# ScalarE norms the fifth tile's x one round sooner, and VectorE takes the sixth tile's statistics behind the shared expert's first activation

## The chip, the cores and the metric

The kernel runs on one core of a Trainium2 chip, in one launch. The metric is the time of an execution in microseconds of the device, the median of several runs. The engines are TensorE (PE, with its weight loads PEld), VectorE (DVE), ScalarE (ACT), GpSimd (POOL) and SyncE (SP), which issues DMAs. They run side by side and wait for each other by semaphores only.

## The reference

The input is x, 16 sequences of 512 tokens, 128 wide, in float32. Cut to what is computed:

```python
y  = layernorm(x)                                  # no gain
n1 = layernorm(y) * ln1_g + ln1_b
r, k, v = sigmoid(n1 @ Wr.T), n1 @ Wk.T, n1 @ Wv.T
e   = exp(k - exp(n1 @ Ww.T))
num = scan(decay * num + e * v);  den = scan(decay * den + e)   # along the sequence
a   = y + (r * num / (den + eps)) @ Wo.T
n2  = layernorm(a) * ln2_g + ln2_b
x1  = x + a + sigmoid(n2 @ Wrec.T) * (relu(n2 @ Wkey.T) ** 2 @ Wval.T)
h   = layernorm(x1)
out = x1 + shared_expert(h) + routed_expert(h)     # 1 of 16 experts for each token
```

## The kernel before

A tile is one sequence of 512 tokens, so there are 16 tiles, in four groups of 128 tokens. The first part of the kernel, some 330 us, takes all tiles through the time mix, the channel mix, the router and the shared expert, and scatters the rows by expert into HBM. The second part runs the routed experts on the sorted rows and isn't touched.

In the first part each engine has one program of rounds, `one_round(n)`. In round n the line `for t in at(k)` runs its step for tile t = n - k, so one round holds steps of several tiles, each at its own stage, in an order that is written out by hand. Rounds of different engines are not aligned by anything but the semaphores: `wait(engine, name, t)` waits until the step called `name` is done for tile t. An engine that waits holds back all that is written behind it.

The steps in question, with the lines of the profile, are these.

- VectorE, `stats_of_x(t)`: the mean and variance of x by four BATCH_NORM_STATS2 (L1180, into `stA`) and four BATCH_NORM_AGGREGATE (L1185, into `mvA`). It waits for the load of x. Tiles 0 to 3 are done ahead of the rounds, tile 4 (`EARLY_STATS`) early in round 4, the later ones at `at(0)`, between `so_far` and `ev`.
- GpSimd, the terms of the norm (`pA`, L1650 to L1656), one group of small instructions, first in its round at `at(2)`. Behind them in the same round come `row_ids`, `h_terms` (L1603, L1590, L1592, L1606: the terms of the norm of h, for an older tile), `scaled` (L1616, h times the router's score), the four products `p1`, `p3`, `p0`, `p2` (L1672 to L1678), `xn0`, `sum_a`, `pC` and the scatters (L1630). In the round with `pA(5)`, `h_terms` is of tile 1, `scaled` of tile 0 and the products of tile 3.
- ScalarE, `norm_x(t)`: four activations (L935), one for each group, which write `xn1tok`. It stands second in its round, behind `tanh_of_max`. Later in the round come `copy_a`, `silu1`, `copy_x`, the four `relu`, `gate_tanh`, `norm_h` (L1010), `exp_w` (L1004, behind a load of the table), `copy_h` (L1016) and more. `norm_x(2)` is moved already: it stands behind `exp_w(1)`.
- TensorE, `turn_x(t)`: the transposes of `xn1tok` (L429), which wait for `norm_x(t)`. In the same round follow `gate1`, `up1` (which waits for `ev`), `keys`, `down_first`, `last_key` (L560, which waits for `act1` of the tile two back), the projections of x, `turn_h` (L429 too), the products with Wo (L734 to L745, each of which waits for one of `p1`, `p3`, `p0`, `p2`), `gate0`, `logits`, `up0`, the products with Wval (L435) and at the end the transposes of `an` (L781).
- VectorE in round 5, in order: `norm_a(2)`, the scan of `den(3)` (L1421), `so_far(0)`, `stats_of_x(5)`, `ev(3)` (L1431), `q(3)` (L1436), `act0(0)` (L1333), `mixed(1)` (L1339 to L1343, with the statistics of h), a reciprocal, `act1(0)` (L1354), a reciprocal, the scan of `num(3)` (L1455) and two reciprocals. Round 6 begins with `places(0)` and `k_less_w(4)` (L1274), which waits for `exp_w(4)`.

Of the kernel before, what the change touches and what calls it, by code (L numbers as in the profile page):

```python
# [93 lines left out]
def program(nc, x, w_main, w_exp, vecs, out):  # L94
# [4 lines left out]
    with ExitStack() as ctx:  # L99
# [12 lines left out]
        def wait(eng, name, t, k=None):  # L112

            of = WHO.get(name, range(NT))
            count = sum(1 for u in of if u <= t)
            if count:
                eng.wait_ge(s[name], (count - 1) * PER[name] + (PER[name] if k is None or t not in of else k))
# [88 lines left out]
        def grp(tile, g):  # L206
            return tile[:, g * P:(g + 1) * P]
# [20 lines left out]
        def at_round(n):  # L228


            return lambda behind, of=range(NT): [n - behind] if n - behind in of else []
# [6 lines left out]
        EARLY_STATS, IN_HALVES = 4, 2  # L238
# [630 lines left out]
        def _(act_e):  # L869
# [23 lines left out]
            def tanh_of_max(t):  # L893
                wait(act_e, "mx", t)
                wait(act_e, "sc", t - 2)
                af(ths[t % 2][:, :], mx[t % 2][:, :], ACT.Tanh, scale=0.5).then_inc(s["ths"], 1)
# [19 lines left out]
            def silu1(t):  # L916
                wait(act_e, "G1", t)
                wait(act_e, "ac1", t - 1)
                af(sgA[1][:, :], bank[4][:, :], ACT.Silu).then_inc(s["sg1"], 1)

            def copy_a(t):
                if t < IN_HALVES:
                    for half in range(2):
                        wait(act_e, "T2", t, half + 1)
                        af(xn2T[t % 2][:, half * HALF:(half + 1) * HALF], T2_of(t, half)[:, half * HALF:(half + 1) * HALF], ACT.Identity,
                           bias=V("b2"), scale=V("g2")).then_inc(s["xn2T"], 1)
                else:
                    wait(act_e, "T2", t)
                    af(xn2T[t % 2][:, :], T2_B[:, :], ACT.Identity, bias=V("b2"), scale=V("g2")).then_inc(s["xn2T"], 2)  # L929

            def norm_x(t):
                wait(act_e, "pA", t)
                wait(act_e, "T1", t - 2)
                for g in range(G if t else 1):
                    ins = af(grp(xn1tok[t % 2], g), grp(xin[t % XR], g), ACT.Identity, bias=smA[t % 3][:, 5, g:g + 1],  # L935
                             scale=smA[t % 3][:, 4, g:g + 1])
                ins.then_inc(s["xn1tok"], 1)

            def copy_x(t):
                act_e.wait_ge(s["T1"], t + 1)  # L940
                af(xn1T[t % 2][:, :], T1_B[:, :], ACT.Identity, bias=V("b1"), scale=V("g1")).then_inc(s["xn1T"], 1)

            def exp_r(t):
                act_e.wait_ge(s["Rp"], t + 1)
                wait(act_e, "q", t - 2)
                af(er[t % 2][:, :], R_B[:, :], ACT.Exp, scale=-1.0).then_inc(s["er1"], 1)
# [9 lines left out]
            def relu0(t):  # L956
                act_e.wait_ge(s["K0"], t + 1)
                wait(act_e, "k20", t - 1)
                af(kr[0][:, :], KE_BANK[0][:, :], ACT.Relu).then_inc(s["kr0"], 1)

            def relu2(t):
                wait(act_e, "K2", t)
                wait(act_e, "k22", t - 1)
                af(kr[2][:, :], KE_BANK[2][:, :], ACT.Relu).then_inc(s["kr2"], 1)

            def relu1(t):
                wait(act_e, "K1", t)
                wait(act_e, "k21", t - 1)
                af(kr[1][:, :], KE_BANK[1][:, :], ACT.Relu).then_inc(s["kr1"], 1)

            def relu3(t):
                wait(act_e, "K3", t)
                wait(act_e, "k23", t - 1)
                af(kr[3][:, :], KE_BANK[3][:, :], ACT.Relu).then_inc(s["kr3"], 1)  # L974

            def square0(t):
                wait(act_e, "kr0", t)
                wait(act_e, "VAL0", t - 1)
                af(k2[0][:, :], kr[0][:, :], ACT.Square).then_inc(s["k20"], 1)
# [16 lines left out]
            def gate_tanh(t):  # L996
                wait(act_e, "REC", t)
                wait(act_e, "rv", t - 2)
                af(th[t % 2][:, :], REC_B[:, :], ACT.Tanh, scale=0.5).then_inc(s["th"], 1)

            def exp_w(t):
                wait(act_e, "Wp", t)
                wait(act_e, "e", t - 2)
                af(ew[t % 2][:, :], W_B[:, :], ACT.Exp).then_inc(s["ew"], 1)  # L1004
# [18 lines left out]
            def one_round(n):  # L1023
                at = at_round(n)
                for t in at(6):
                    tanh_of_max(t)
                for t in at(2):
                    if t != 2:
                        norm_x(t)
                for t in at(4):  # L1030
                    copy_a(t)
                    if t == 0:
                        exp_r(t + 2)
                for t in at(6, A_TILES):
                    silu1(t)
                for t in at(6, B_TILES):
                    wait(act_e, "hG0", t)
                    wait(act_e, "hac0", t - 1)
                    af(sgB[0][:, :], bank[2][:, :], ACT.Silu).then_inc(s["hsg0"], 1)
                for t in at(2):  # L1040
                    if t != 2:
                        copy_x(t)
                for t in at(6, B_TILES):
                    wait(act_e, "hG1", t)
                    wait(act_e, "hac1", t - 1)
                    af(sgB[1][:, :], bank[4][:, :], ACT.Silu).then_inc(s["hsg1"], 1)
                for t in at(4):
                    relu0(t)
                    relu2(t)
                    relu1(t)  # L1050
                    gate_tanh(t)
                for t in at(4):
                    if t == 1:
                        relu3(t)
                        square0(t)
                for t in at(2):
                    if t == 3:
                        exp_w(t)
                for t in at(5):
                    norm_h(t)  # L1060
                for t in at(2):
                    if t - 4 in A_TILES:
                        nc.scalar.preload_act_table(ACT.Exp)
                    if t not in (2, 3):
                        exp_w(t)
                    if t == 1:
                        norm_x(t + 1)
                for t in at(5):
                    copy_h(t)
                for t in at(4):  # L1070
                    if t != 1:
                        relu3(t)
                        square0(t)
                for t in at(2):
                    if t != 1:
                        exp_z(t)
                for t in at(4):
                    square2(t)
                for t in at(2):
                    if t == 1:  # L1080
                        copy_x(t + 1)
                    if t != 2:
                        exp_r(t)
                for t in at(4):
                    square1(t)
                for t in at(2):
                    one_more(t)
                    if t == 1:
                        exp_w(t + 1)
                        exp_z(t)  # L1090
                for t in at(4):
                    square3(t)
                for t in at(5, A_TILES):
                    silu0(t)
# [69 lines left out]
        def _(dve):  # L1164
# [97 lines left out]
            def stats_of_x(t):  # L1262
                dve.wait_ge(s[f"x_in{t % XR}"], 16 * (t // XR + 1))
                wait(dve, "agA", t - 2)
                bn_stats_of(stA[t % 2], lambda g: grp(xin[t % XR], g), "agA")
                wait(dve, "agA", t, 1)
                wait(dve, "pA", t - 3)
                wait(dve, "xn1tok", t - 3)
                bn_aggr_of(mvA[t % 3], stA[t % 2], "agA")
# [60 lines left out]
            def act0(t):  # L1330
                wait(dve, "sg0", t)
                wait(dve, "U0", t)
                v.tensor_tensor(actA[0][:, :], sgA[0][:, :], bank[3][:, :], ALU.mult).then_inc(s["ac0"], 1)  # L1333
# [36 lines left out]
            def one_round(n):  # L1370
                at = at_round(n)
# [50 lines left out]
                for t in at(5):  # L1422
                    so_far(t)
                for t in at(0):
                    if t > EARLY_STATS:
                        stats_of_x(t)
                for t in at(2):
                    wait(dve, "e", t)
# [7 lines left out]
                    v.scalar_tensor_tensor(q[t % 2][:, :], den[t % 2][:, :], WKV_EPS, er[t % 2][:, :], ALU.add, ALU.mult).then_inc(s["q"], 1)  # L1436
                for t in at(5, A_TILES):
                    act0(t)
                for t in at(4):
                    mixed(t)  # L1440
                for t in at(2):
# [328 lines left out]
```

## Time and profile before

| | |
|---|---|
| median of 3 runs | 484.36 us (484.09 to 484.52) |
| the profiled execution, its time | 484.58 us |
| the profiled execution, its span | 482.9 us |
| PE busy | 472.7 us, 98% |
| DVE, ACT, POOL busy | 371.4, 324.2 and 352.6 us |

The span is that of the instructions; the execution's own time holds 1.68 us more around it. A busy PE is not PE at its peak, since matmuls are pipelined. The chain of work that ended last lies on PE for 84% of the span. Times in rows are counted from the start of the span. A releaser in brackets is the instruction whose end let the waiting one start.

### The profile page before, as it was taken

The numbers are of one execution on the slowest core, as the hardware profiler recorded it, in microseconds if no ns is written. First come the engines' busy times: TensorE is split into PE (matmuls) and PEld (weight loads), VectorE is DVE, ScalarE is ACT, GpSimd is POOL, SyncE is SP. The second block draws the span as 40 slices with busy tenths as digits, with TensorE's granted clock in tenths as the row PEclk, the third lists the DMA queues.
The fourth block names the chain that finished last, engine by engine and source line by source line (L and its number), as shares of the span: only waits on it lengthen the run. The fifth ranks groups of instructions, "written<-read, shape, count | busy, mean of one in ns | idle before, by whom it ended". The sixth has DMA issues, their size and how long they took to land.

```text
span 482.9 us, 10368 instructions
## 1 busy us (share of the span) xinstructions
PE 472.7 (98%) x3025; PEld 383.6 (79%) x3025; DVE 371.4 (77%) x1076; ACT 324.2 (67%) x625; POOL 352.6 (73%) x571
## 2 busy tenths in 40 slices
PE   8999999999999999999999999999999999999997
PEld 7556677868777778686777868877889999999996
DVE  7899899999999999996899989847545455555426
ACT  2777887987978879777687986563265555565421
POOL 6667498898898988986798877767326777767750
PEclk9999999999999999999999999999999999999999
DMA  7052001102102011010101001011489855542028
GB/s 240 2 191 115 1 23 44 56 12 67 34 33 68 23 45 56 12 66 24 44 24 46 33 12 46 33 42 39 121 187 246 229 167 150 150 130 72 23 68 282
DMA packets 33031, 39.32 MB, mean 81 GB/s; under 512 B 4913, under 2 KB 29113, under 8 KB 32720
## 3 DMA queue, kind: packets, MB, share of 16 engines
q1 hardware_dynamic: 26640, 24.98, 18.1%
q0 software_dynamic: 5760, 13.16, 7.8%
q8 instruction: 25, 0.41, 0.4%
q10 hardware_dynamic: 576, 0.52, 0.3%
q14 instruction: 30, 0.25, 0.2%
HBM read 21.69 MB, written 17.93 MB: 82 GB/s over the span
## 4 chain that ended last, share of the span: by engine, by line
PE 84%; DVE 6%; issue 3%; DMA 2%; ACT 2%; POOL 2%; SPq 1%; DVEq 0%; POOLq 0%; ACTq 0%
PE bank L442 20%; PE bank L435 11%; PE bank L459 6%; PE bank L450 4%; PE bank L850 4%; PE bank L858 3%; PE bank L857 3%; PE bank L548 3%; PE bank L560 3%; PE bank L544 3%; PE bank L539 3%; PE bank L429 3%; PE bank L534 2%; PE bank L605 2%; PE bank L619 2%
## 5 line engine op out<-in xcount | busy, mean ns | idle before, releaser
L442 PE MATMUL bank<-hT,wm 128*128 128x256 f32 x512 | 124.7, 383 | 0.6 <-ACT kr L974 0.6
L442 PEld LDWEIGHTS bank<-hT,wm 128*128 128x128 f32 x512 | 92.0, 190 | 18.7 <-issue 8.5
L1630 POOL DMA_INDIRECT sorted_rows<-rows,posi x64 | 72.8, 1138 | 20.1 <-issue 16.9
L1725 POOL DMA_INDIRECT out<-shared x55 | 53.2, 967 | 36.2 <-DVE shared L1542 22.7
L435 PEld LDWEIGHTS bank<-wm,k 128*128 128x128 f32 x512 | 61.7, 192 | 8.0 <-issue 6.4
L435 PE MATMUL bank<-wm,k 128*128 128x128 f32 x512 | 62.4, 275 | 0.1
L1153 ACT ACTIVATE er<-bank 128x256 f32<-128x256 f32 x40 | 15.3, 383 | 41.6 <-PE bank L858 40.9
L1550 DVE TENSOR_TENSOR e<-er,bank 128x256 f32<-128x256 f32 x40 | 16.8, 421 | 22.5 <-ACT er L1153 18.9
L459 PE MATMUL bank<-wm,actA 128*128 128x128 f32 x240 | 32.9, 280 | 0.0
L1010 ACT ACTIVATE h<-rows,smE 128x128 f32<-128x128 f32 x64 | 26.3, 482 | 8.1 <-POOL smE L1606 8.0
L459 PEld LDWEIGHTS bank<-wm,actA 128*128 128x128 f32 x240 | 29.3, 192 | 0.2 <-issue 0.2
L1725 POOL DMA_INDIRECT out<-rows x24 | 23.2, 965 | 7.8 <-issue 5.2
L1683 POOL TENSOR_SCALAR shared<-shared,smA 128x128 f32<-128x128 f32 x64 | 27.9, 448 | 0.0
L935 ACT ACTIVATE xn1tok<-shared,smA 128x128 f32<-128x128 f32 x61 | 25.0, 481 | 2.8 <-POOL smA L1646 2.8
L1616 POOL TENSOR_SCALAR rows<-h,sc 128x128 f32<-128x128 f32 x64 | 25.4, 412 | 1.6
L1654 POOL TENSOR_TENSOR smA<-smA,half 128x8 f32<-128x8 f32 x15 | 25.0, 1666 | 1.3
L1542 DVE TENSOR_TENSOR shared<-bank,shared 128x256 f32<-128x256 f32 x28 | 11.8, 422 | 16.4 <-PE bank L850 16.4
L548 PEld LDWEIGHTS bank<-wm,xn2T 128*128 128x128 f32 x128 | 16.8, 192 | 7.7 <-issue 7.7
L1621 POOL TENSOR_TENSOR xa<-shared,a 128x512 f32<-128x512 f32 x16 | 20.4, 1274 | 2.8 <-DVE rows L1343 1.9
L929 ACT ACTIVATE xn2T<-bank,vec 128x512 f32<-128x512 f32 x14 | 10.9, 777 | 15.4 <-PE bank L781 15.4
L1421 DVE TENSOR_TENSOR_SCAN den<-decay,e 128x512 f32<-128x512 f32 x16 | 19.4, 1211 | 0.3 <-ACT e L950 0.3
L1190 DVE TENSOR_SCALAR an<-a,mvC,smC 128x128 f32<-128x128 f32 x64 | 18.4, 380 | 0.7 <-POOL smC L1692 0.6
(267 smaller groups left out, 1289.5 us busy)
## 6 DMA issues: line engine op xcount, KB each, us to landing
shared<-sorted_rows SPq DMA_DIRECT2D x56, 128.5 KB, 3.4
shared<-x SPq DMA_DIRECT2D x16, 256.0 KB, 2.8
rows<-sorted_rows SPq DMA_DIRECT2D x24, 128.5 KB, 2.4
wexp<-w_exp SPq DMA_DIRECT2D x2, 1536.0 KB, 8.6
sorted_rows<-filler SPq DMA_DIRECT2D x17, 128.5 KB
shared<-out SPq DMA_DIRECT2D x6, 256.0 KB
out<-shared SPq DMA_DIRECT2D x12, 128.0 KB, 2.2
sorted_rows<-rows,posi POOLq DMA_INDIRECT x64
```

The costliest lines, as they stand in the source:

```text
L435: ins = mm(grp(acc, g), grp(lhs, g), W(name, f), start=(f == 0 and g == 0), stop=(f == F // P - 1), skip_group_check=True)
L442: ins = mm(dst[:, j * HALF:(j + 1) * HALF], W(name, 2 * pair_ + j), src[:, half * HALF:(half + 1) * HALF], start=True, stop=True)
L459: ins = mm(grp(acc, 2 * half + g), lhs[:, at_:at_ + P], W("down", 2 * pair_ + j), start=(pair_ == 0 and j == 0 and g == 0), stop=(pair_ == ...
L548: ins = mm(grp(REC_B, g), grp(xn2T[t % 2], g), W("Wrec"), start=True, stop=True)
L935: ins = af(grp(xn1tok[t % 2], g), grp(xin[t % XR], g), ACT.Identity, bias=smA[t % 3][:, 5, g:g + 1], scale=smA[t % 3][:, 4, g:g + 1])
L1010: ins = af(grp(h[t % 2], g), base_of(t)[:, g, :], ACT.Identity, bias=smE[t % 3][:, 3, g:g + 1], scale=smE[t % 3][:, 1, g:g + 1])
L1616: ins = g_.tensor_scalar(rows[t % 3][:, g, 0:D], grp(h[t % 2], g), sc[t % 2][:, g:g + 1], 1.0, ALU.mult, ALU.mult)
L1621: g_.tensor_tensor(xa[t % 3][:, :], xin[t % XR][:, :], a[t % 2][:, :], ALU.add).then_inc(s["xa"], 1)
L1630: g_.indirect_dma_start(sorted_ap, bass.IndirectOffsetOnAxis(posi[t % 3][:, g:g + 1].bitcast(U32), 0), rows[t % 3][:, g, :], None).then_in ...
L1654: g_.tensor_tensor(sm[:, 3:5, :], sm[:, 1:3, :], half8[:, :, :], ALU.pow).then_inc(s["pA"], 1)
L1683: ins = g_.tensor_scalar(grp(xn0[t % 4], g), grp(xin[t % XR], g), smA[t % 3][:, 0, g:g + 1], smA[t % 3][:, 3, g:g + 1], ALU.add, ALU.mult)
L1725: g_.indirect_dma_start(out, bass.IndirectOffsetOnAxis(xr[k % RING][:, j, D:D + 1].bitcast(U32), 0), xr[k % RING][:, j, D + 1:ROW], None, ...
```

## The change

On ScalarE, `norm_x(4)` is taken out of its place at the head of round 6. It is put into round 5, where t of `at(2)` is 3: behind `norm_h(0)` and ahead of `copy_h(0)`, at the place where `norm_x(2)` stands in round 3. On VectorE, `stats_of_x(5)` is taken out of its place ahead of `ev(3)` in round 5 and put behind `act0(0)`, ahead of `mixed(1)`. No instruction is added or removed. All other tiles keep their places.

```diff
@@ ScalarE, one_round
                 for t in at(2):
-                    if t != 2:
+                    if t not in (2, 4):
                         norm_x(t)
@@
                     if t not in (2, 3):
                         exp_w(t)
-                    if t == 1:
+                    if t in (1, 3):
                         norm_x(t + 1)
@@ VectorE, one_round
                 for t in at(0):
-                    if t > EARLY_STATS:
+                    if t > EARLY_STATS + 1:
                         stats_of_x(t)
@@
                 for t in at(5, A_TILES):
                     act0(t)
+                for t in at(0):
+                    if t == EARLY_STATS + 1:
+                        stats_of_x(t)
                 for t in at(4):
                     mixed(t)
```

## Rows read from the trace of the kernel before

**Rows 1.** The page: busy time of PE and PEld, and its granted clock by slices.

```profile
PE 472.7 (98%) x3025; PEld 383.6 (79%) x3025; DVE 371.4 (77%) x1076; ACT 324.2 (67%) x625; POOL 352.6 (73%) x571
PEclk9999999999999999999999999999999999999999
```

**Rows 2.** Timeline of PE: start us, us, engine, line, op, out<-in, count, [idle before].

```profile
55.56 0.66 PE L429 MATMUL bank<-ident,xn1tok 128*128 128x128 f32 x4 [1.04 <-ACT xn1tok L935]
...
62.20 1.02 PE L560 MATMUL bank<-xn2T,wm 128*128 128x512 f32 x2
...
66.92 0.41 PE L745 MATMUL bank<-wm,q 128*128 128x128 f32 x2
...
75.18 0.60 PE L429 MATMUL bank<-ident,xn1tok 128*128 128x128 f32 x4
...
94.66 0.60 PE L429 MATMUL bank<-ident,xn1tok 128*128 128x128 f32 x4
```

**Rows 3.** Timeline of ACT.

```profile
45.35 1.65 ACT L1010 ACTIVATE h<-rows,smE 128x128 f32<-128x128 f32 x4 [0.41 <-POOL smE L1606]
48.21 0.60 ACT L1016 ACTIVATE hT<-bank 128x512 f32<-128x512 f32 x1 [1.21 <-PE bank L429]
...
62.54 1.65 ACT L1010 ACTIVATE h<-rows,smE 128x128 f32<-128x128 f32 x4 [0.44 <-POOL smE L1606]
...
82.59 1.65 ACT L1010 ACTIVATE h<-rows,smE 128x128 f32<-128x128 f32 x4 [0.98 <-POOL smE L1606]
...
92.71 1.64 ACT L935 ACTIVATE xn1tok<-shared,smA 128x128 f32<-128x128 f32 x4
```

**Rows 4.** Timeline of DVE.

```profile
49.16 0.69 DVE L1388 TENSOR_TENSOR a<-bank,shared 128x512 f32<-128x512 f32 x1 [1.23 <-PE bank L745]
...
54.92 0.84 DVE L1180 BATCH_NORM_STATS2 stA<-shared 128x6 f32<-128x128 f32 x4
...
56.10 0.65 DVE L1431 TENSOR_TENSOR ev<-e,bank 128x512 f32<-128x512 f32 x1
...
57.87 0.68 DVE L1339 SCALAR_TENSOR_TENSOR rv<-th,bank 128x512 f32<-128x512 f32 x1
...
61.35 0.63 DVE L1354 TENSOR_TENSOR actA<-sgA,bank 128x512 f32<-128x512 f32 x1
...
62.75 1.16 DVE L1455 TENSOR_TENSOR_SCAN num<-decay,ev 128x512 f32<-128x512 f32 x1
...
66.74 0.68 DVE L1274 TENSOR_TENSOR ew<-bank,ew 128x512 f32<-128x512 f32 x1
...
81.41 1.16 DVE L1455 TENSOR_TENSOR_SCAN num<-decay,ev 128x512 f32<-128x512 f32 x1
...
86.25 0.69 DVE L1274 TENSOR_TENSOR ew<-bank,ew 128x512 f32<-128x512 f32 x1 [0.75 <-ACT ew L1004]
...
100.65 1.16 DVE L1455 TENSOR_TENSOR_SCAN num<-decay,ev 128x512 f32<-128x512 f32 x1
```

**Rows 5.** Timeline of POOL.

```profile
60.69 0.19 POOL L1603 TENSOR_SCALAR smE<-mvE 128x4 f32<-128x4 f32 x1 [1.15 <-DVE mvE L1185]
...
62.30 0.20 POOL L1606 TENSOR_TENSOR smE<-smE 128x4 f32<-128x4 f32 x1
...
62.76 2.37 POOL L1616 TENSOR_SCALAR rows<-h,sc 128x128 f32<-128x128 f32 x4
...
66.35 0.45 POOL L1678 TENSOR_TENSOR q<-num,q 128x128 f32<-128x128 f32 x1
...
80.64 1.02 POOL L1592 TENSOR_TENSOR smE<-smE,half 128x4 f32<-128x4 f32 x1
81.74 0.82 POOL L1606 TENSOR_TENSOR smE<-smE 128x4 f32<-128x4 f32 x1
...
82.82 1.41 POOL L1616 TENSOR_SCALAR rows<-h,sc 128x128 f32<-128x128 f32 x4
...
85.44 0.46 POOL L1678 TENSOR_TENSOR q<-num,q 128x128 f32<-128x128 f32 x1
```

## The prediction, made before the changed kernel was run

> **What bounds the kernel now.** I read the page's totals first, then one timeline per engine of the rounds around the change, from 45 to 100 us, and asked of each row of TensorE what released it. TensorE is busy for 98% of the span, and its granted clock is full in every slice, which is the upper of its two levels, 2.4 GHz [rows 1]. So a saving can only be a gap of TensorE, and a loss only a new one. In the stretch that the change touches there is one gap: 1.04 us ahead of the transposes of the fifth tile's x (tile 4), which end when ScalarE's norm of that tile lands [rows 2]. From then on TensorE runs in rounds of 19.48 us (75.18 to 94.66) without an idle note. The question is thus what TensorE meets next when this gap is closed. The reader is to see three thin margins in the rows. The last key product (L560) starts at 62.20 and needs `act1` of tile 0, which VectorE ends at 61.35 + 0.63 = 61.98 [rows 2, 4]. The last product of the time mix (L745) starts at 66.92 and needs GpSimd's product that ends at 66.35 + 0.45 = 66.80 [rows 2, 5]. The transposes of tile 5 start at 75.18 and need the norm of that tile, the 10th to 12th microsecond behind `norm_h` on ScalarE [rows 2, 3].
>
> **The change on ScalarE.** `norm_x(4)`, four activations, 1.64 us in the row of the same kind at 92.71 [rows 3], leaves the head of round 6 and goes behind `norm_h(0)` in round 5, ahead of `copy_h(0)`. `norm_h(0)` runs 45.35 to 47.00, and `copy_h(0)` started at 48.21 behind 1.21 us of waiting for its transposes. So 1.21 of the 1.64 us lie in idle time, and `copy_h(0)` starts at 48.64 by durations, 0.43 later. Successive activations of this engine start about 0.1 before the record of the last one ends, twice here, so I take 0.23. All that TensorE does behind the gate product of tile 0 slips by these 0.2, up to the gap. If the cover were gone, the whole 1.64 would fall on TensorE there. Behind it the gap of 1.04 closes, so TensorE stands 1.04 - 0.23 = 0.81 ahead of before (between 0.61 and 1.04).
>
> **The change on VectorE.** `stats_of_x(5)` takes 56.10 - 54.92 = 1.18 us. It goes from before `ev`, `q` and `act0` to behind them. `ev(3)`, for which the second up product of tile 0 waits, then starts at 54.92 instead of 56.10. That is needed, since TensorE is now early. The three instructions that pass in front take 57.87 - 56.10 = 1.77 us. The sum on VectorE is nought: `mixed(1)` still starts at 57.87. VectorE had its last idle time before 49.16 and shows none until 86.25 [rows 4], so it cannot follow TensorE forward: `act1(0)` still ends at 61.98. TensorE waits there for it. The lead of 0.81 shrinks to at most 62.20 - 61.98 = 0.22, less what passes between release and start, about 0.1. So some 0.7 of the gap comes back as a wait in front of L560, whatever else is true.
>
> **What queues behind the later statistics.** On GpSimd the terms of tile 5's norm (`pA`) stand ahead of `h_terms(1)`, `scaled(0)` and the four products `p1`, `p3`, `p0`, `p2`. The statistics end 1.77 later, so `pA` starts 1.77 later. `h_terms(1)` began at 60.69 behind 1.15 us of idle time [rows 5]. It begins at 60.69 - 1.15 + 1.77 = 61.31 now. Its last instruction (L1606) started 1.61 behind its first (62.30 - 60.69) and so starts at 62.92. That is a new meeting. VectorE's scan of `num` runs from 62.75 to 63.91 [rows 4]. In the row before, L1606 took 0.20 us and was over before the scan. In the next round it started at 81.74, inside a scan that ran 81.41 to 82.57, and took 0.82, to 82.56 [rows 4, 5]. So L1606 ends at about 63.91, not 62.50, and `norm_h(1)` on ScalarE starts at 63.94 instead of 62.54, 1.40 later.
>
> Part of this is paid already: `scaled(0)` (L1616) took 2.37 us at 62.76, under the scan, and 1.41 in the next round, behind it. It now starts as there, 82.82 - 81.74 - 0.82 = 0.26 behind the end of L1606, at 64.17. From its start to the end of `p2` the next round has 85.44 + 0.46 - 82.82 = 3.08 us [rows 5]. `p2` ends at 67.25 instead of 66.80. L745 cannot start before about 67.29, which is 0.37 later than before. The tenth that was left of the lead is spent too.
>
> **What is late next.** In the next round ScalarE started `norm_x(6)` at 92.71, 10.12 behind `norm_h(2)` at 82.59, with VectorE's `k_less_w` 3.66 behind it at 86.25 [rows 3, 4]. From 63.94 this gives `k_less_w(4)` at 67.60 instead of 66.74 (VectorE 0.86 late), and `norm_x(5)` from 74.06 to 75.70. TensorE, 0.37 late, would start the transposes of tile 5 at 75.55, and now waits until about 75.76: 0.58 later than at 75.18.
>
> A round on, VectorE's scan stands at 81.41 + 0.86 = 82.27. The same steps (13.01 from scan to transposes, 75.76 - 62.75) give 95.28 against 75.76 + 19.48 = 95.24, another 0.04. From scan to scan this loop needs 100.65 - 81.41 = 19.24, less than TensorE's 19.48, so it recovers 0.24 a round and the loss stays at about 0.6. Nothing behind gives it back, since TensorE has no gaps to spend. The sum: gap closed -1.04, `copy_h` +0.23, wait for `act1` +0.7, wait for `p2` +0.48, wait for `norm_x(5)` +0.21, together +0.58. I forecast 484.58 + 0.58 = 485.16 for an execution like the profiled one, and 484.36 + 0.58 = 484.94 for the median. The profiled execution (span 482.9) was 0.22 above the median. The case's own range is 484.6 to 485.3: 0.2 less if the wait for `norm_x(5)` is covered, and up to 0.4 more if L745 also waits on an extended `p2`.
>
> **A rule against the trace.** In the next round GpSimd's L1592 ran from 80.64 to 81.66, and the scan started under it at 81.41 and took 1.16 like the one at 62.75 [rows 4, 5]: VectorE is not seen held by the instruction that came first. The Trainium skill (SBUF — State Buffer, Who interferes with whom) says of the pair of ports that VectorE and GpSimd share: "Whoever issues first gets the shared pair for the whole instruction"; a scan with two inputs in SBUF would have to wait for a reading GpSimd instruction that is ahead. By it the sum would be that of rival 2 below; by the row it is mine.
>
> **The rivals.**
> 1. GpSimd gets through before the scan. L1606 is due at 62.92, 0.17 behind the scan's start. Were the terms of tile 5 or `h_terms(1)` 0.2 to 0.4 shorter than before, L1606 would take 0.20 and L1616 would meet the scan as before, `p2` ending at 66.8 again. TensorE then keeps 0 to 0.1 of its lead: 484.3 to 484.4. For it: the margin is small. Against it: the length of the same work is the same in all rounds read. Chance 0.17.
> 2. The scan is held by L1592. L1592 starts 1.10 ahead of L1606 (81.74 - 80.64) and lasts 1.02, so here it would run from 61.82 to 62.84, over the start of the scan due at 62.75. If the scan waits for its end, it and all behind it come 0.09 later: 484.36 + 0.58 + 0.09 = 485.03. Against it stands the scan at 81.41, which started under L1592 and took its usual time. Chance 0.06.
> 3. Slower. `scaled(0)` keeps its 2.37 us wherever it runs, because what stretched it was VectorE's reciprocals and not the scan. Then `p2` ends at 67.25 + 0.96 = 68.21, L745 starts at 68.25, and TensorE is 1.33 late from there on: 485.69. It decides from a stretch of 0.6 us on. For it: the first of these rows covers both kinds. Against it: at 82.82, under reciprocals alone, it takes 1.41. Chance 0.12.
> 4. Faster. The lead of 0.81 survives because `act1(0)` and `p2` move forward too. This needs VectorE itself to run 0.8 sooner between 49.16 and 61.35, so a wait hidden in its rows that TensorE's lead removes. It gives 484.36 - 0.81 = 483.55. VectorE's rows follow each other without a gap there, which speaks against it. Chance 0.07.
>
> **How the numbers follow.** My forecast has the other 0.58. A measurement of this kernel tells about 0.2% (0.97 us) from no change. Of my cases only the fourth rival is faster by that, only the third slower, and I give 0.03 of the forecast's chance to a sum that runs over 0.97. So faster 0.07, within 0.2% 0.78, slower 0.15. Cases of both signs lie close around no change. The range leaves out the third and fourth rival, 0.19 together: from 484.1, which is rival 1 with 0.2 for runs apart, to 485.5, the forecast's upper end with the same.
>
> **What the changed kernel's profile would show.** TensorE's transposes of tile 4 without a wait near 54.6 (right for the first step). L560 at 62.0 to 62.1, its weights released by `act1`; if it stands near 61.3, rival 4 is true. GpSimd's L1606 of tile 1 with 0.8 to 1.0 us, ending at 63.9, and L1616 behind it with 1.41; 0.20 there means rival 1, over 2 us rival 3. L745 at 67.3, and the transposes of tile 5 at 75.7 to 75.8 with a wait for `norm_x(5)`. The prediction fails if VectorE does not keep its times up to 62.75, or if the last rounds or the experts' part, which I take as unchanged, shift by themselves.

## The result, and the profile after

The changed kernel takes 485.18 us in the median of 13 runs (484.68 to 485.97), the kernel before 484.36 us in its 13 (483.97 to 484.67). The ratio is 1.0017, with a 95% interval of 1.0009 to 1.0025. So the change costs between 0.4 and 1.2 us. That is clear of noise, but small: the median is 0.24 us above the forecast of 484.94 and inside the range.

The profiled execution took 484.97 us, with a span of 483.2 us. It started 0.30 us later than the one before, ahead of everything that was changed: the transposes of tile 0's h, which stood at 47.57, stand at 47.87. In the profiles below this point differs by up to 1.5 us. So in this text a corrected time is a time of a trace less the shift of these transposes against 47.57.

TensorE's timeline of the changed kernel (start us, us, engine, line, what, count, idle before) answers [rows 2].

```profile
47.87 0.60 PE L429 MATMUL bank<-ident,h 128*128 128x128 f32 x4
...
54.87 0.60 PE L429 MATMUL bank<-ident,xn1tok 128*128 128x128 f32 x4
...
62.38 1.10 PE L560 MATMUL bank<-xn2T,wm 128*128 128x512 f32 x2 [0.82 <-issue]
...
67.60 0.49 PE L745 MATMUL bank<-wm,q 128*128 128x128 f32 x2
...
76.06 0.66 PE L429 MATMUL bank<-ident,xn1tok 128*128 128x128 f32 x4
...
95.59 0.60 PE L429 MATMUL bank<-ident,xn1tok 128*128 128x128 f32 x4
```

The gap of 1.04 us is gone: the transposes of tile 4 stand at 54.57 corrected instead of 55.56, 0.99 earlier. The next row shows where it went: 0.82 us of waiting in front of L560. The row names no releaser; `act1(0)` ended 0.09 us ahead of its start, and `e3` and `e7` below show that it is the one. L745 stands at 67.30 corrected (66.92 before), the transposes of tile 5 at 75.76 (75.18) and those of tile 6 at 95.29 (94.66). From there the difference of 0.63 us holds through all later tiles: the last transposes of `an` in the first part stand at 312.06 against 311.13, 0.63 after the correction.

The two profiled executions do not keep this difference to their end. VectorE's last instruction starts at 479.74 before and at 480.10 now, 0.06 after the correction. In the second part the kernel before waited once for a DMA that brings the sorted rows, and the changed kernel shows no such wait:

```profile
358.87 0.44 PE L841 MATMUL bank<-ident,shared 128*128 128x128 f32 x2 [0.35 <-DMA shared<-sorted_rows]
```

Of the other profiles four have this wait too (0.19 to 0.24 us), and the rest show none. So one execution's end says little about a change of this size. The medians and the starts in the first part carry the comparison.

GpSimd's timeline of the changed kernel answers [rows 5]. Lines of GpSimd are three higher now: L1609 is L1606 of before, L1619 is L1616, L1681 is L1678. So are those of VectorE behind `act0`: L1458 is L1455.

```profile
58.38 0.19 POOL L1653 TENSOR_SCALAR smA<-mvA 128x4 f32<-128x4 f32 x1 [5.53 <-DVE mvA L1185]
...
61.72 0.19 POOL L1606 TENSOR_SCALAR smE<-mvE 128x4 f32<-128x4 f32 x1
...
63.34 0.87 POOL L1609 TENSOR_TENSOR smE<-smE 128x4 f32<-128x4 f32 x1
...
64.47 1.41 POOL L1619 TENSOR_SCALAR rows<-h,sc 128x128 f32<-128x128 f32 x4
...
67.09 0.45 POOL L1681 TENSOR_TENSOR q<-num,q 128x128 f32<-128x128 f32 x1
```

The 1.15 us of idle time ahead of `h_terms(1)` are gone, and the small product took 0.87 us instead of 0.20. VectorE's rows beside it, and ScalarE's:

```profile
61.66 0.63 DVE L1354 TENSOR_TENSOR actA<-sgA,bank 128x512 f32<-128x512 f32 x1
...
63.06 1.16 DVE L1458 TENSOR_TENSOR_SCAN num<-decay,ev 128x512 f32<-128x512 f32 x1
...
67.91 0.69 DVE L1274 TENSOR_TENSOR ew<-bank,ew 128x512 f32<-128x512 f32 x1 [0.75 <-ACT ew L1004]
```

```profile
64.25 1.65 ACT L1010 ACTIVATE h<-rows,smE 128x128 f32<-128x128 f32 x4 [2.94 <-POOL smE L1609]
...
74.36 1.64 ACT L935 ACTIVATE xn1tok<-shared,smA 128x128 f32<-128x128 f32 x4
```

The small product ends at 64.21, with the scan at 64.22. ScalarE waited 2.94 us for it, 0.44 before [rows 3]. `act1(0)` stands at 61.36 corrected, where it stood before [rows 4].

### The profile page after: what moved, and what is told of

The parts are those of the page before. It is cut to its first block, busy times and chain, and to the rows that moved or that the text cites. A ratio compares the mean times of both kernels' runs of the same rounds, so it can differ in the third digit from the quotient of the medians.

```text
span 483.2 us, 10368 instructions
## 1 busy us (share of the span) xinstructions
PE 472.8 (98%) x3025; PEld 383.3 (79%) x3025; DVE 371.0 (77%) x1076; ACT 324.1 (67%) x625; POOL 352.6 (73%) x571
## 4 chain that ended last, share of the span: by engine, by line
PE 87%; DVE 6%; issue 2%; POOL 2%; ACT 1%; DMA 1%; DVEq 0%; POOLq 0%; ACTq 0%
PE bank L442 21%; PE bank L435 11%; PE bank L459 6%; PE bank L450 5%; PE bank L857 4%; PE bank L858 4%; PE bank L850 4%; PE bank L548 3%; PE bank L560 3%; PE bank L544 3%; PE bank L539 3%; PE bank L429 3%; PE bank L534 2%; PE bank L605 2%; PE bank L619 2%; PE bank L724 2%
## 5 line engine op out<-in xcount | busy, mean ns | idle before, releaser
L442 PE MATMUL bank<-hT,wm 128*128 128x256 f32 x512 | 124.7, 383 | 0.6 <-ACT kr L974 0.6
L442 PEld LDWEIGHTS bank<-hT,wm 128*128 128x128 f32 x512 | 92.1, 190 | 18.8 <-issue 8.1
L1619 POOL TENSOR_SCALAR rows<-h,sc 128x128 f32<-128x128 f32 x64 | 24.5, 398 | 1.6
```

The costliest lines, as they stand in the source:

```text
L442: ins = mm(dst[:, j * HALF:(j + 1) * HALF], W(name, 2 * pair_ + j), src[:, half * HALF:(half + 1) * HALF], start=True, stop=True)
L1619: ins = g_.tensor_scalar(rows[t % 3][:, g, 0:D], grp(h[t % 2], g), sc[t % 2][:, g:g + 1], 1.0, ALU.mult, ALU.mult)
```

## The experiments

All runs below have five rounds against the kernel before, on the same chip as the others of their group: `e1` to `e4`, `e5` to `e7`, `e8` to `e10`, `e11` and `e12`. Each ratio is against the kernel before in the same group. The edits are shown against the changed kernel. The corrected times of TensorE are put together at the end of this section.

**One part of the change at a time.** `e1_scalar_only` leaves VectorE as before, `e2_vector_only` leaves ScalarE as before.

```diff
                 for t in at(0):
-                    if t > EARLY_STATS + 1:
+                    if t > EARLY_STATS:
                         stats_of_x(t)
...
-                for t in at(0):
-                    if t == EARLY_STATS + 1:
-                        stats_of_x(t)
```

> ScalarE's part of the change alone: norm_x(4) behind norm_h(0), VectorE as before. My theory (the loss comes from the later statistics on VectorE, through GpSimd and the scan): the transposes of tile 4 start about 54.6 without a gap, L560 waits for act1 to about 62.05, L745 and the transposes of tile 5 stand where they stood before or 0.1 sooner; 484.2 to 484.4 us. Rival (the later copy_h and the fuller ScalarE row cost the time): the transposes of tile 5 are late by 0.6 with this part alone; 485.0 to 485.2 us.

Measured: 484.29 us, ratio 0.9996 (0.9987 to 1.0005). The time is as I expected, the place of the wait is not. The gap closes, and most of it is lost again two products later, at the second up product, which waits 0.87 us for `ev(3)`. L560 then stands at its old time, 62.20, without a wait:

```profile
54.49 0.60 PE L429 MATMUL bank<-ident,xn1tok 128*128 128x128 f32 x4
...
56.83 1.10 PE L442 MATMUL bank<-hT,wm 128*128 128x256 f32 x4 [0.87 <-DVE ev L1431]
...
75.12 0.60 PE L429 MATMUL bank<-ident,xn1tok 128*128 128x128 f32 x4
```

```diff
                 for t in at(2):
-                    if t not in (2, 4):
+                    if t != 2:
                         norm_x(t)
...
-                    if t in (1, 3):
+                    if t == 1:
                         norm_x(t + 1)
```

> VectorE's part alone: stats_of_x(5) behind act0(0), ScalarE as before. My theory: the gap of 1.04 ahead of the transposes of tile 4 stays, L1606 of tile 1 takes 0.8 to 1.0 us in the scan, L745 at 67.3 and the transposes of tile 5 at 75.76 (counted on the start of the before), so all of the loss is here; 484.9 to 485.2 us. Rival (ScalarE's part costs): as before, 484.3 to 484.5 us.

Measured: 485.0 us, ratio 1.0013 (1.0003 to 1.0022). The gap stays, and tile 5 comes at 75.76 corrected, as in the full change:

```profile
55.48 0.66 PE L429 MATMUL bank<-ident,xn1tok 128*128 128x128 f32 x4 [1.05 <-ACT xn1tok L935]
...
67.22 0.49 PE L745 MATMUL bank<-wm,q 128*128 128x128 f32 x2
...
75.67 0.66 PE L429 MATMUL bank<-ident,xn1tok 128*128 128x128 f32 x4
```

The whole loss comes with VectorE's part. ScalarE's part costs nothing and, alone, gains nothing that a time shows.

**Statistics ahead instead of behind.** `e3_both_stats_ahead` keeps ScalarE's part and puts `stats_of_x(5)` where VectorE was idle for 1.23 us, ahead of the sum `a(2)` in the same round [rows 4]. `e4_stats_ahead_only` does that without ScalarE's part. The edit is that of `e3`.

```diff
+                for t in at(0):
+                    if t == EARLY_STATS + 1:
+                        stats_of_x(t)
                 for t in at(3):
                     wait(dve, "TM2", t)
...
                 for t in at(5, A_TILES):
                     act0(t)
-                for t in at(0):
-                    if t == EARLY_STATS + 1:
-                        stats_of_x(t)
```

> ScalarE's part, and stats_of_x(5) not behind act0(0) but ahead of the sum a(2) in round 5, where VectorE had 1.2 us of idle time. My theory: VectorE is 1.18 us ahead from ev(3) on, act1(0) ends near 60.8, L1606 of tile 1 starts near 61.1, ahead of the scan, and takes 0.20, so TensorE keeps its lead of 0.7 to 0.8 at L560, L745 and the transposes of tile 5; 483.5 to 483.8 us. Rival (TensorE's lead is lost to something else, so a closed gap is worth nothing): 484.2 to 484.5 us.

Measured: 483.53 us, ratio 0.9980 (0.9971 to 0.9989), faster than both kernels. My range was 483.5 to 483.8. The lead is kept at each of the three places, 0.89 us at all of them:

```profile
54.57 0.60 PE L429 MATMUL bank<-ident,xn1tok 128*128 128x128 f32 x4
...
61.31 1.02 PE L560 MATMUL bank<-xn2T,wm 128*128 128x512 f32 x2
...
66.03 0.42 PE L745 MATMUL bank<-wm,q 128*128 128x128 f32 x2
...
74.29 0.60 PE L429 MATMUL bank<-ident,xn1tok 128*128 128x128 f32 x4
```

```profile
59.80 0.19 POOL L1606 TENSOR_SCALAR smE<-mvE 128x4 f32<-128x4 f32 x1 [4.39 <-DVE mvE L1185]
...
61.42 0.20 POOL L1609 TENSOR_TENSOR smE<-smE 128x4 f32<-128x4 f32 x1
```

> stats_of_x(5) ahead of the sum a(2), ScalarE as before. My theory: VectorE and GpSimd are early but the gap of 1.04 ahead of the transposes of tile 4 stays, so TensorE gains nothing to 0.1; 484.2 to 484.4 us. Rival (it is VectorE's row that bounds the rounds, and ScalarE's norm only fills time): 483.5 to 483.8 us.

Measured: 484.44 us, ratio 1.0002 (0.9993 to 1.0011). VectorE and GpSimd are as early as in the run before (`h_terms(1)` at 59.80 in both), and TensorE still has its gap of 1.04 and gains 0.08. So both are needed: the norm early, and VectorE early. Either alone is worth nothing that a time shows.

**A smaller and a larger delay of the statistics.** `e6_stats_behind_ev` puts `stats_of_x(5)` behind `ev(3)` and ahead of `q(3)`. `e7_stats_behind_act1` puts it behind `act1(0)`.

```diff
                     v.tensor_tensor(ev[t % 2][:, :], e[t % 2][:, :], V_B[:, :], ALU.mult).then_inc(s["ev"], 1)
+                for t in at(0):
+                    if t == EARLY_STATS + 1:
+                        stats_of_x(t)
...
-                for t in at(0):
-                    if t == EARLY_STATS + 1:
-                        stats_of_x(t)
```

> The changed kernel with stats_of_x(5) behind ev(3) but ahead of q(3), so that the statistics end 0.6 us later than in the kernel before and not 1.8. My theory: this fits into GpSimd's 1.15 us of idle time ahead of h_terms(1), L1606 takes 0.20 as before, L560 still waits for act1 to about 62.05, and the transposes of tile 5 stand at 75.1 to 75.2; 484.2 to 484.4 us. Rival (the loss grows with every delay of the statistics): a third of the loss, 484.6 us.

Measured: 484.62 us against 484.61 of the kernel before in this group, ratio 0.9999 (0.9990 to 1.0008). The idle time ahead of `h_terms(1)` shrank from 1.15 to 0.64 us and took the delay up, and `h_terms(1)` starts at its old time (60.69 corrected). So a delay of 0.6 us, inside that reserve, is free.

```profile
62.17 0.19 POOL L1606 TENSOR_SCALAR smE<-mvE 128x4 f32<-128x4 f32 x1 [0.64 <-DVE mvE L1185]
...
63.78 0.20 POOL L1609 TENSOR_TENSOR smE<-smE 128x4 f32<-128x4 f32 x1
```

```diff
                     act0(t)
-                for t in at(0):
-                    if t == EARLY_STATS + 1:
-                        stats_of_x(t)
...
                     act1(t)
+                for t in at(0):
+                    if t == EARLY_STATS + 1:
+                        stats_of_x(t)
```

> The changed kernel with stats_of_x(5) further back, behind mixed(1) and act1(0). VectorE's act1(0) is then 1.2 us earlier, so TensorE may keep its lead at L560. My theory (what counts is GpSimd's queue: the terms of tile 5 stand ahead of h_terms(1) and all products): the terms start at 62.0 instead of 56.3, L1606 ends at 67.1, p2 ends near 70.4, the transposes of tile 5 come near 79.0, 3.8 us late; 488.0 to 488.4 us. Rival (VectorE's act1 is what takes TensorE's lead, GpSimd's queue has room): faster than the kernel before, 483.6 to 484.0 us.

Measured: 489.78 us in the median of 4 runs, ratio 1.0109 (1.0093 to 1.0124), outside my range. The queue is right and the size is short by 1.6 us. TensorE keeps its lead at L560 (61.09 corrected) and then stands still for 4.45 us, until `norm_h(1)`, which waits behind the terms of tile 5:

```profile
69.10 0.66 PE L429 MATMUL bank<-ident,h 128*128 128x128 f32 x4 [4.45 <-ACT h L1010]
...
70.92 0.64 PE L745 MATMUL bank<-wm,q 128*128 128x128 f32 x2
71.35 1.91 PE L612 MATMUL bank<-xn1T,wm 128*128 128x512 f32 x2
```

What my sum had left out stands in the stretches of this run (core 0: us, then busy time and count of PE, PEld, DVE, ACT and POOL, the granted clock, DMA):

```profile
64.60:69.10 4.50, 0.05 (x1) 0.00 (x1) 1.73 (x6) 1.68 (x5) 4.09 (x13) 1.00 0.00 0
69.10:70.00 0.90, 0.90 (x7) 0.79 (x7) 0.00 (x0) 0.90 (x1) 0.90 (x3) 0.98 0.00 0
70.00:71.00 1.00, 1.00 (x5) 1.00 (x6) 0.00 (x0) 0.99 (x3) 1.00 (x3) 0.50 0.08 16
71.00:72.00 1.00, 1.00 (x4) 0.69 (x4) 0.94 (x3) 1.00 (x3) 1.00 (x4) 0.50 0.00 0
72.00:73.00 1.00, 1.00 (x2) 0.34 (x1) 0.96 (x4) 1.00 (x3) 1.00 (x2) 0.50 0.00 0
73.00:74.00 1.00, 1.00 (x5) 0.72 (x3) 0.72 (x6) 1.00 (x3) 0.80 (x2) 0.81 0.00 0
```

The granted clock was still full when the work began again, and fell to its lower level, 1.2 GHz, for some 3 us from about 70.0 on. The two products of L612 took 1.91 us instead of the 1.02 that such a pair takes elsewhere. From L745 to the transposes of tile 5 this run needs 9.45 us, the kernel before 8.26 [rows 2]: 1.19 of the missing 1.6 us. The rest is on GpSimd: `p2` ended at 70.91 corrected and not near 70.4. There the power instruction of tile 5 was held by the scan (2.46 us instead of 1.64).

**Taking the collision with the scan away.** `e5_scan_first` moves the scan of `num(3)` ahead of a reciprocal. GpSimd's product `p3` needs that reciprocal and gets a wait for it.

```diff
                 for t in at(2):
-                    wait(dve, "q", t)
-                    v.reciprocal(grp(q[t % 2], 3), grp(q[t % 2], 3))
+                    if t != 3:
+                        wait(dve, "q", t)
+                        v.reciprocal(grp(q[t % 2], 3), grp(q[t % 2], 3))
...
+                    if t == 3:
+                        wait(dve, "q", t)
+                        v.reciprocal(grp(q[t % 2], 3), grp(q[t % 2], 3))
...
+                    if t == 3:
+                        wait(gp, "rq0", t)
                     g_.tensor_tensor(grp(q[t % 2], 3), grp(num[t % 2], 3), grp(q[t % 2], 3), ALU.mult).then_inc(s["p3"], 1)
```

> The changed kernel, with VectorE's scan of num(3) ahead of its reciprocal of group 3 instead of behind it, so that the scan runs from about 61.9 to 63.06 instead of 62.75 to 63.91 (times counted on the start of the before). GpSimd's products still have what they need by the time they are due. My theory (the loss is the meeting of L1606 of tile 1 with the scan): L1606, due at 62.92, is held to about 63.1 only, norm_h(1) starts near 63.15, L745 near 66.9, the transposes of tile 5 at 75.2, and the time is 484.2 to 484.5 us. Rival (the lateness of h_terms by 0.6 costs by itself, whoever holds the port): L745 at 67.1 or later and 484.7 to 485.1 us.

Measured: 485.24 us, ratio 1.0016 (1.0006 to 1.0025), so neither theory's sum. The experiment did not do what it was made for. An earlier scan (62.09 to 63.30) met the power instruction one place ahead. L1599 and L1613 here are L1595 and L1609 of the changed kernel:

```profile
62.15 1.96 POOL L1599 TENSOR_TENSOR smE<-smE,half 128x4 f32<-128x4 f32 x1
64.18 0.20 POOL L1613 TENSOR_TENSOR smE<-smE 128x4 f32<-128x4 f32 x1
```

It took 1.96 us instead of 1.01, and the small product behind it is later than in the changed kernel (63.99 corrected against 63.04). The hold moved to the instruction in front. This run says nothing on how much of the loss is the hold.

**Two branches.** Behind `h_terms(1)` the lateness goes two ways: over `p2` to L745, and over `norm_h(1)`, ScalarE's row and `norm_x(5)` to the transposes of tile 5. `e8_products_first` puts the four products of tile 3 ahead of `scaled(0)` on GpSimd. `e9_h_terms_first` puts the last product of tile 5's terms and `row_ids(2)` behind `h_terms(1)`. `e10_both_orders` does both.

```diff
                 for t in at(7):
-                    scaled(t)
+                    if t != 0:
+                        scaled(t)
...
+                for t in at(7):
+                    if t == 0:
+                        scaled(t)
                 for t in at(3):
                     wait(gp, "pA", t)
```

> The changed kernel, with GpSimd's four products of tile 3 ahead of scaled(0) in that round. This takes the lateness of p2 away but not that of L1606, which still meets the scan. Times counted on the start of the before. My theory (each of two branches behind h_terms(1) is enough by itself: p2 for 0.4 to 0.5, the norm of tile 5 for 0.58): L745 at 66.8 or sooner, norm_h(1) still at 63.94, the transposes of tile 5 still at 75.76 and waiting for norm_x(5); 484.9 to 485.2 us. Rival (L745 is what costs, the norm of tile 5 only fills the wait): 484.2 to 484.5 us.

Measured: 485.05 us, ratio 1.0012 (1.0003 to 1.0021). L745 is free (66.87 corrected), and the transposes of tile 5 still come at 75.74, now with their own wait in the row. So the branch of `norm_x(5)` costs 0.56 at tile 5 by itself:

```profile
66.78 0.39 PE L745 MATMUL bank<-wm,q 128*128 128x128 f32 x2
...
75.65 0.65 PE L429 MATMUL bank<-ident,xn1tok 128*128 128x128 f32 x4 [0.29 <-ACT xn1tok L935]
```

```diff
-                        wait(gp, "pA", t, 2)
-                        g_.tensor_tensor(sm[:, 5, :], sm[:, 0, :], sm[:, 4, :], ALU.mult).then_inc(s["pA"], 1)
+                        if t != 5:
+                            wait(gp, "pA", t, 2)
+                            g_.tensor_tensor(sm[:, 5, :], sm[:, 0, :], sm[:, 4, :], ALU.mult).then_inc(s["pA"], 1)
...
                     h_terms(t)
+                for t in at(2):
+                    if t == 5:
+                        sm = smA[t % 3]
+                        wait(gp, "pA", t, 2)
+                        g_.tensor_tensor(sm[:, 5, :], sm[:, 0, :], sm[:, 4, :], ALU.mult).then_inc(s["pA"], 1)
+                for t in at(5):
+                    if t == 2:
+                        row_ids(t)
```

> The changed kernel, with the last small product of tile 5's terms and row_ids(2) behind h_terms(1) on GpSimd, so that L1606 starts near 62.6, just ahead of the scan (62.75). It takes the hold off L1606, and the next small instruction takes it instead. My theory: L1606 takes 0.20, norm_h(1) starts at 62.9, the transposes of tile 5 do not wait for norm_x(5), but p2 ends near 67.4, L745 comes at 67.5 and the transposes of tile 5 at 75.7; 484.8 to 485.1 us. Rival (the hold of L1606 is the whole of the loss): 484.2 to 484.5 us.

Measured: 484.99 us, ratio 1.0012 (1.0003 to 1.0021). The time is in my range, but the premise failed: the small product started 0.11 us ahead of the scan (63.27 and 63.38 in this trace) and was held all the same. It took 1.26 us, so `norm_h(1)` was late too, and this run does not part the branches.

> Both orders of GpSimd together in the changed kernel: L1606 ahead of the scan and the products ahead of scaled(0). My theory: both branches are free, L560 still waits for act1 to about 62.05, L745 near 66.8, the transposes of tile 5 at 75.0 to 75.2, and the whole loss is gone; 484.2 to 484.4 us. Rival (something else that came with the later statistics costs the time): 484.8 us or more.

Measured: 485.08 us, ratio 1.0016 (1.0007 to 1.0025), outside my range. The same hold (1.26 us), so only the branch of `p2` was freed, and the run repeats `e8`: L745 at 66.88, tile 5 at 75.75.

So two more runs start the small product 0.4 us ahead of the scan, by moving the negated mean of tile 5 behind `h_terms(1)` too. `e12_h_terms_earlier` has this with the products in their place, `e11_both_orders_earlier` with the products ahead.

```diff
                     else:
-                        g_.tensor_scalar(sm[:, 0, :], mvA[t % 3][:, :, 0], -1.0, 0.0, ALU.mult, ALU.add)
+                        if t != 5:
+                            g_.tensor_scalar(sm[:, 0, :], mvA[t % 3][:, :, 0], -1.0, 0.0, ALU.mult, ALU.add)
...
                 for t in at(6):
                     h_terms(t)
+                for t in at(2):
+                    if t == 5:
+                        sm = smA[t % 3]
+                        g_.tensor_scalar(sm[:, 0, :], mvA[t % 3][:, :, 0], -1.0, 0.0, ALU.mult, ALU.add).then_inc(s["pA"], 1)
+                        wait(gp, "pA", t, 2)
+                        g_.tensor_tensor(sm[:, 5, :], sm[:, 0, :], sm[:, 4, :], ALU.mult).then_inc(s["pA"], 1)
```

> The same without the other order of the products: scaled(0) stays ahead of them. My theory: L1606 takes 0.20 and norm_h(1) starts at 62.6, so the transposes of tile 5 do not wait for norm_x(5), but an instruction behind L1606 is held by the scan instead, p2 ends near 67.4, L745 comes at 67.5 and the transposes of tile 5 at 75.7: the p2 branch alone costs 0.5; 484.8 to 485.1 us. Rival (the norm of tile 5 is the only branch that costs): 484.2 to 484.5 us.

Measured: 484.89 us, ratio 1.0013 (1.0005 to 1.0022). Now the premise holds: the small product took 0.20 us, `norm_h(1)` started at 62.60 corrected, and `norm_x(5)` was done at 74.72, a whole microsecond before it was needed. L745 came at 67.45 and tile 5 at 75.78, so the branch of `p2` alone costs 0.5 at L745 and 0.6 at tile 5. The instruction behind the small product, L1681 here, was held to the scan's end in its place:

```profile
62.32 0.20 POOL L1609 TENSOR_TENSOR smE<-smE 128x4 f32<-128x4 f32 x1
...
62.76 1.11 POOL L1681 TENSOR_TENSOR smA<-smA 128x4 f32<-128x4 f32 x1
```

> As the run with both orders of GpSimd, but the negated mean of tile 5's terms (L1653 in the changed kernel) also goes behind h_terms(1), so that L1606 of tile 1 starts near 62.3, 0.4 ahead of the scan (62.75), where it was still held with 0.1 to spare. Times counted on the start of the before. My theory (two branches, p2 and the norm of tile 5, and nothing else): L1606 takes 0.20, norm_h(1) starts at 62.6, L745 near 66.8, the transposes of tile 5 at 75.0 to 75.2; the whole loss is gone, 484.2 to 484.5 us. Rival (something else that came with the later statistics costs the time): 484.8 us or more.

Measured: 485.26 us, ratio 1.0019 (1.0010 to 1.0028). Half of my theory held: L745 stands at 66.89 and the transposes of tile 5 at 75.12, so at that place the loss is gone. The time did not come back. One round on, the transposes of tile 6 are at 95.37, 0.71 late. VectorE shows the way:

```profile
72.31 1.12 DVE L1190 TENSOR_SCALAR an<-a,mvC,smC 128x128 f32<-128x128 f32 x4 [0.48 <-POOL smC L1595]
...
82.49 1.16 DVE L1458 TENSOR_TENSOR_SCAN num<-decay,ev 128x512 f32<-128x512 f32 x1
```

`norm_a(3)` waits for GpSimd's terms of `a`, which stand behind `scaled(0)` and `xn0(4)`. From there VectorE is 0.96 late (its scan at 82.37 corrected, 81.41 before [rows 4]), GpSimd's next small product is held until that scan ends, and the same two branches are late in the next round. The rival, that something else costs the time, is true to this extent: there is a third branch, and it is GpSimd's queue again.

Part of the 0.71 is this run's own doing. The products stand earlier in it, and the last of them waited for VectorE's reciprocal. GpSimd stood idle there in `e8` (0.36) and `e10` (0.22) too:

```profile
65.78 0.46 POOL L1696 TENSOR_TENSOR q<-num,q 128x128 f32<-128x128 f32 x1 [0.36 <-DVE q L1462]
```

The terms of `a` come later by that too. In `e12`, which has no such wait, `norm_x(6)` was done at 94.95, where `e11` had it at 95.32. As an estimate from these rows, the third branch would bring tile 6 at about 95.0, 0.3 late, and the other 0.4 comes from the new order of the products. No run shows the third branch alone.

Starts on TensorE, corrected by the transposes of tile 0's h, with the median and the ratio. Medians of different groups are not to be compared, the ratios are:

| kernel | tile 4 | L560 | L745 | tile 5 | tile 6 | median us | ratio |
|---|---|---|---|---|---|---|---|
| before | 55.56 | 62.20 | 66.92 | 75.18 | 94.66 | 484.36 | 1 |
| changed | 54.57 | 62.08 | 67.30 | 75.76 | 95.29 | 485.18 | 1.0017 |
| e1, ScalarE only | 54.57 | 62.20 | 66.93 | 75.20 | 94.68 | 484.29 | 0.9996 |
| e2, VectorE only | 55.57 | 62.15 | 67.31 | 75.76 | 95.30 | 485.00 | 1.0013 |
| e3, statistics ahead | 54.57 | 61.31 | 66.03 | 74.29 | 93.77 | 483.53 | 0.9980 |
| e4, ahead, VectorE only | 55.57 | 62.15 | 66.87 | 75.10 | 94.58 | 484.44 | 1.0002 |
| e5, scan first | 54.56 | 62.09 | 67.58 | 76.04 | 95.57 | 485.24 | 1.0016 |
| e6, behind `ev` | 54.57 | 62.08 | 66.88 | 75.19 | 94.67 | 484.62 | 0.9999 |
| e7, behind `act1` | 54.57 | 61.09 | 71.14 | 80.59 | 100.06 | 489.78 | 1.0109 |
| e8, products first | 54.55 | 62.08 | 66.87 | 75.74 | 95.37 | 485.05 | 1.0012 |
| e9, `h_terms` first | 54.55 | 62.08 | 67.58 | 75.91 | 95.39 | 484.99 | 1.0012 |
| e10, both | 54.55 | 62.08 | 66.88 | 75.75 | 95.38 | 485.08 | 1.0016 |
| e11, both, earlier | 54.57 | 62.09 | 66.89 | 75.12 | 95.37 | 485.26 | 1.0019 |
| e12, `h_terms` earlier | 54.56 | 62.08 | 67.45 | 75.78 | 95.26 | 484.89 | 1.0013 |

The column of tile 6 orders the kernels as the medians do, up to what the ratios' intervals (about 0.1% either way, 0.45 us) can tell.

## Why the prediction was right

It was right in direction and in its main steps. The size is right too, with one step right by luck and two terms off that did not matter:

- The gap closes and TensorE leads. Forecast 0.81, measured 0.99. The `copy_h(0)` part (0.2 late) was right: the transposes of `an` ahead of the gap stand at 54.14 corrected, 0.22 late. But the gap's 1.04 was counted from the end of the transposes in front, and consecutive transposes follow each other at 0.43 from start to start (0.60 is the time of one group), so the lead is 0.17 larger. It made no difference, as the next wait takes all but a tenth: 0.87 instead of the 0.7 of the sum.
- L560 waits for `act1(0)`. Forecast 62.0 to 62.1, measured 62.08, with 0.82 us of waiting. `e3` and `e7`, in which `act1(0)` is earlier, have L560 at 61.31 and 61.09: this step is shown.
- The later statistics go through GpSimd. Forecast for the first instruction of `h_terms(1)` 61.31, measured 61.42 corrected. The tenth came from one of tile 5's terms (L1655, 0.75 us), held by VectorE's two-input instruction at 58.89.
- The small product meets the scan, and `norm_h(1)` starts at 63.94. Measured 63.95. L745 forecast 67.29, measured 67.30.
- Tile 5 at 75.76. Measured 75.76.
- Tile 6 at 95.28, 0.62 late. Measured 95.29 and 0.63, but not by the step that the prediction gives, so this number is luck. The prediction has VectorE 0.86 late at the next scan (82.27). It was 0.87 late at `k_less_w(4)` and only 0.49 at that scan (81.90), since two short waits before it, 0.16 us for TensorE's logits and 0.21 for GpSimd's terms of `a`, took up the rest. The rows of before carry them without an idle note, and I had read VectorE as having none. `norm_x(6)` was done at 94.90, so the transposes of tile 6 did not wait for it. The extra 0.05 lies in those of tile 5: they had waited and took 0.49 from their start to the next product, not 0.44.
- The loss then stays to the end of the first part, as forecast. The reason given, that TensorE has no gaps to spend, is too strong: both kernels have one of 0.60 in front of L442 (226.14 before). It kept its length, so it gave nothing back. In the second part the waits for DMAs differ from one execution to the next, as said above.

The first rival (GpSimd before the scan) did not come true in the changed kernel. `e12` brings the small product ahead of the scan in another way, by moving two small instructions behind it, and the loss is the same, by `p2`. The rival's own condition, terms shorter by 0.2 to 0.4 us, no run has. Of the delay only 0.62 us lie beyond the reserve, so by an estimate from the rows `p2` would still be 0.2 to 0.4 late, and the 0 to 0.1 that I let TensorE keep looks too kind. The third rival is refuted by `scaled(0)` at 1.41 us, the fourth by `act1(0)` at its old time. For the second, the scan started at 63.06 under the power instruction (62.26 to 63.27) and took its 1.16, so nothing speaks for it.

What was too simple is the sum's last part. I wrote it as a chain, 0.48 for `p2` and 0.21 for `norm_x(5)`. `e8` and `e12` show that these are two ways side by side, each of which costs about 0.6 at tile 5 by itself. `e11` shows a third one, over VectorE's `norm_a(3)`, when both are free. This one had no margin before the change either: GpSimd's terms of `a` ended at 71.19 and `norm_a(3)` started at 71.23.

The cause is thus not one collision. GpSimd's queue has next to no idle time behind `h_terms(1)`, and at three places what leaves it is needed at once. The statistics came 1.77 later, 1.15 of that was idle time, and the other 0.62 is the size of the loss. That the sizes agree is no proof by itself, but `e6` (0.6 late, no loss) and `e7` (5.8 late, so 4.7 beyond the reserve, and L745 4.2 late) fit it. How much of the loss each branch would cost without the scan's hold stays open: no run removed the hold from the queue, only from one instruction.

The medians differ by 0.82 us, the starts in the first part by 0.63. The interval of the ratio, 0.4 to 1.2 us, covers both, and the other 0.2 is not explained.

## What to carry to other kernels

A gap on the busiest engine is worth what its next supplier lets through: look up, for each of its following waits, how long before the need the supplier was done, and take the smallest. When a step is moved back on one engine, find the engine that waits for it and read the idle time in front of the work that stands behind that wait. This reserve (1.15 us here) is what the move may take for nothing: 0.6 us was free, 1.77 was not. And if a step must move, look for idle time ahead of it first: the same 1.18 us of statistics, put into VectorE's idle 1.23 us instead of behind the activation, turned a loss of 0.17% into a gain of 0.20%.

## What the runs showed of the hardware

- Engines of this kernel do not wait for each other by semaphores only, as the first section has it. A short GpSimd instruction that reads SBUF is held to the end of a VectorE instruction with two SBUF inputs, even if its start is up to 0.11 us ahead. In the changed kernel L1655 started at 58.88, VectorE's L1343 at 58.89, and L1655 took 0.75 us instead of 0.19. In `e9` the small product started 0.11 us ahead of the scan and took 1.26 instead of 0.20. In these meetings VectorE's scan took 1.16 us (1.21 in `e5`) and its L1343 0.69. Alone, in the kernel before, they took 1.16 (at 16.95) and 0.69 (at 40.58). The rows of `e9`, GpSimd and then VectorE:

```profile
63.27 1.26 POOL L1609 TENSOR_TENSOR smE<-smE 128x4 f32<-128x4 f32 x1
```

```profile
63.38 1.16 DVE L1458 TENSOR_TENSOR_SCAN num<-decay,ev 128x512 f32<-128x512 f32 x1
```

- A longer GpSimd instruction was held as well when the scan started 0.06 us ahead of it (`e5`: 1.96 us instead of 1.01). When it started 0.8 us ahead of the scan, it was not, and neither was the scan: 1.01 and 1.16 us in the changed kernel, at 62.26 and 63.06.
- The Trainium skill (SBUF — State Buffer, Who interferes with whom) has the instruction that issues first keep the ports and the other wait. The runs do not bear this out as the profile gives the starts: of instructions 0.01 and 0.11 us apart it was the first that waited, and VectorE was not seen waiting, not even 0.8 us behind. Whether the profile's start is that of the issue stays open.
- After 4.45 us without work TensorE's granted clock fell to 1.2 GHz, 0.9 us after the work began again and for some 3 us (`e7`), which made a lateness of 4.2 us at L745 one of 5.4 at tile 5.
- The same instruction, ahead of anything that the change or the edits delay, starts up to 1.5 us apart in two profiles (47.57 before, 49.05 in `e6`). Compare stretches from a common instruction on, not from the start of the span.
